# Channel gate of a convolutional block: wider matmuls for the two sums over pixels, and a one-byte throw-away output

## The reference

```
xn   = group_norm(x, 32 groups of 16 channels)
r    = relu(xn)
r    = where(max_pixels(r) - mean_pixels(r) < 0.5, 0, r)
bb   = 1 - exp(-|max_channels(r) - mean_channels(r)|)      # one value per pixel
y    = bb * r
x_max, pooled = max_pixels(y), mean_pixels(y)
c1   = sigmoid(pooled @ W1.T);  c3 = relu(pooled @ W3.T);  c3 = where(c3 < 1, 1.2, c3)
out  = x + where(y < c1 * c3 * x_max, 0, y)
```

## Time and profile before

| | |
|---|---|
| device time, median of 3 runs | 1788.29 us (1784.95 to 1790.47) |
| the profiled execution, its own time | 1780.24 us |
| its span in the trace | 1778.4 us |
| mean granted TensorE clock | 0.843 of 2.4 GHz |
| instructions in the trace | 45243, of these 19616 matmuls and 19616 weight loads |
| mean DMA rate | 292 GB/s |

### The profile page before, as it was taken

How to read it: one execution, slowest core, us unless ns; L and a number is a source line. 1 busy time by engine, 2 the same in 40 slices (tenths; PEclk the granted TensorE clock), 3 DMA queues, 4 the chain that set the end, 5 groups by cost and what they waited for, 6 DMA issues and landing times.

```text
span 1778.4 us, 45243 instructions
## 1 busy us (share of the span) xinstructions
PE 1303.4 (73%) x19616; PEld 1080.2 (61%) x19616; DVE 1460.9 (82%) x2192; ACT 1306.6 (73%) x1921; POOL 610.6 (34%) x446
## 2 busy tenths in 40 slices
PE   4888776788876778767688777678777688777761
PEld 3766655666665666655576655566655566656660
DVE  2588887988887988888888887888887887888987
ACT  5678777777787878777767787777787767777821
POOL 0043233443233444223443233443233442233430
PEclk8898888998888898888888888898878887888885
DMA  9259989999999899998989999989999988899973
GB/s 396 87 162 301 319 315 320 281 296 297 312 330 336 277 285 306 302 329 320 287 263 296 307 330 332 283 277 296 301 330 329 279 265 269 315 329 343 296 228 145
DMA packets 93418, 518.86 MB, mean 292 GB/s; under 512 B 10272, under 2 KB 10272, under 8 KB 93216
## 3 DMA queue, kind: packets, MB, share of 16 engines
q1 hardware_dynamic: 75360, 416.38, 58.4%
q0 software_dynamic: 17856, 99.56, 28.7%
HBM read 310.38 MB, written 205.52 MB: 290 GB/s over the span
## 4 chain that ended last, share of the span: by engine, by line
PE 29%; POOL 26%; ACT 22%; DVE 15%; issue 7%; DMA 1%; SPq 0%; DVEq 0%; ACTq 0%; POOLq 0%
POOL xs L778 23%; ACT rs L476 8%; PE ps_turn L286 7%; PE ps_gate L347 7%; ACT xs L476 7%; PE ps_gate L322 6%; PE ps_gate L294 6%; DVE xs L670 6%; ACT rs L451 5%; DVE rs L670 4%; DVE max_and_mean L622 2%; POOL rstd L757 2%; DMA xs<-in_x 1%; PE ps_gate L356 1%; DVE xs L737 1%
## 5 line engine op out<-in xcount | busy, mean ns | idle before, releaser
L622 DVE TENSOR_REDUCE max_and_mean<-ps_turn 128x2 f32<-128x1024 f32 x384 | 466.0, 1220 | 201.3 <-PE ps_turn L286 200.6
L286 PE MATMUL ps_turn<-ident,xs 128*128 128x128 f32 (+1 forms) x1600 | 358.8, 310 | 177.7 <-DVE max_and_mean L622 112.3
L769 POOL DMA_DIRECT2D xs<-in_x x124 | 111.6, 968 | 940.0 <-DVE xs L670 837.0
L778 POOL TENSOR_TENSOR xs<-xs,rs 128x1568 f32<-128x1568 f32 x124 | 433.3, 3531 | 1.9 <-DVE rs L670 1.9
L286 PEld LDWEIGHTS ps_turn<-ident,xs 128*128 128x128 f32 (+1 forms) x1600 | 204.5, 153 | 311.5 <-DVE max_and_mean L622 155.2
L312 PE MATMUL ps_gate<-ident,bb 128*128 128x128 f32 (+1 forms) x1600 | 273.4, 333 | 153.2 <-ACT bb L469 144.0
L425 ACT ACTIVATE scratch<-xs 128x3136 bf16<-128x3136 f32 x128 | 360.2, 2814 | 7.8 <-DMA xs<-in_x 2.8
L312 PEld LDWEIGHTS ps_gate<-ident,bb 128*128 128x128 f32 (+1 forms) x1600 | 249.6, 239 | 173.4 <-DVE ymax_parts L639 157.7
L286 PE MATMUL ps_turn<-ident,rs 128*128 128x128 f32 (+1 forms) x1600 | 341.3, 299 | 6.0 <-issue 6.0
L639 DVE CUSTOM_DVE_ANT_0 xs<-xs,ps_gate 128x768 f32<-128x768 f32 (+1 forms) x256 | 243.3, 959 | 45.1 <-PE ps_gate L312 45.0
L451 ACT ACTIVATE xs<-xs,shift,rstd 128x3136 f32<-128x3136 f32 x64 | 191.9, 2999 | 100.0 <-POOL shift L761 93.3
(11 more groups left out here) (80 smaller groups left out, 991.9 us busy)
## 6 DMA issues: line engine op xcount, KB each, us to landing
xs<-in_x SPq DMA_DIRECT2D x260, 784.0 KB, 13.7
out<-xs SPq DMA_DIRECT2D x256, 784.0 KB, 8.2
xs<-in_x POOLq DMA_DIRECT2D x124, 784.0 KB, 11.1
rs<-in_L_conv_W SPq DMA_DIRECT2D x2, 1024.0 KB, 18.7
```

The lines of the kernel that those rows point to most:

```text
L286: mm = pe.transpose(ps_turn[0:w, n % 2, b - 2 * i, P * t:P * (t + 1)], r_tile(s, t)[:, P * b:P * b + w], ident[:, :])
L622: ins = dve.tensor_reduce(max_and_mean[:, 2 * i:2 * i + 2, 0], ps_turn[:, n % 2, :, :], AX.X, ALU.max)
L778: pool.tensor_tensor(o, o, half(r_tile(s - 1, t), h), ALU.add).then_inc(added, 1)
```

## The change

`sum_x` takes 448 columns in one matmul instead of 112, so a tile is 7 matmuls and not 28. `mean_rows_of` takes rows of 512 pixels instead of blocks of 128, so a tile is 7 matmuls (the last has 64 columns) and not 25. The four groups of output partitions are used in turn over all 28 matmuls of a sample. Their results lie in the first bank of each half of `ps_gate` or in its second one (`ps_rowsum` in columns 0 to 447 of the second half, `ps_mean_rows` in columns 512 to 1023 of the first), so each step waits for the gates that read these banks, and the wait for `logits_ready` moves from ahead of `sum_x` to `group_stats` and one sample back. `turn_means` becomes four matmuls; ScalarE copies 512 columns of mean rows in place of 128, reads 448 columns of sums in place of 112, and writes the means with a permuted access pattern. `junk` becomes a one-byte tile of its own, and `control_sb` shares memory with the mean rows.

```diff
-XCHUNK = 112
+XCHUNK = 448
+MEAN_ROW = 512
...
-        scratch = sb("scratch", [P, HALF])
-        junk = scratch[:, :].bitcast(BF16)
-        control_sb = scratch[:, 0:C]
+        junk = sb("junk", [P, HW], FP8)
+        rows = sb("rows", [P, C])
+        control_sb = rows[:, :]
+        mean_rows = rows[:, 0:MEAN_ROW]
...
-        ps_mean_rows = small0[:, 0:P]
+        ps_mean_rows = ps_gate[:, 0, 512:512 + MEAN_ROW]
...
-        ps_rowsum = small1[:, 48:48 + XCHUNK]
+        ps_rowsum = ps_gate[:, 1, 0:XCHUNK]
...
             def mean_rows_of(s):
-                for t in range(T):
-                    for b in range(NBLK):
-                        w, k, j = min(P, HW - P * b), b % 4, b // 4
-                        mm = pe.matmul(ps_mean_rows[32 * k:32 * k + 32, 0:w], chan_avg[:, 31 - j:63 - j],
-                                       r_tile(s, t)[:, P * b:P * b + w], start=(t == 0 and b < 4),
-                                       stop=(t == T - 1 and b >= NBLK - 4), skip_group_check=True,
-                                       tile_position=(0, 32 * k))
+                if s > 0:
+                    pe.wait_ge(gated, T * (NG * s - 1))
+                for n in range(T * NM):
+                    t, j, k = n // NM, n % NM, n % 4
+                    w = min(MEAN_ROW, HW - MEAN_ROW * j)
+                    mm = pe.matmul(ps_mean_rows[32 * k:32 * k + 32, 0:w], chan_avg[:, 31 - j:63 - j],
+                                   r_tile(s, t)[:, MEAN_ROW * j:MEAN_ROW * j + w], start=(n < 4),
+                                   stop=(n >= T * NM - 4), skip_group_check=True, tile_position=(0, 32 * k))
                 mm.then_inc(mean_rows_mm, 1)
...
             def turn_means(s):
                 pe.wait_ge(mean_rows_copied, s + 1)
-                pe.matmul(ps_means, mean_rows[:, :], row_block_cols, start=True, stop=True).then_inc(means_mm, 1)
+                for i in range(MEAN_COLS):
+                    mm = pe.matmul(ps_means[:, i, :], mean_rows[:, P * i:P * (i + 1)], row_pick[:, :],
+                                   start=True, stop=True)
+                mm.then_inc(means_mm, 1)
...
             def sum_x(s, tiles):
+                if s > 1:
+                    pe.wait_ge(gated, NG * T * (s - 1))
...
             def group_stats(s):
                 pe.wait_ge(row_mean_ready, s + 1)
+                if s > 1:
+                    pe.wait_ge(logits_ready, s - 1)
...
                 mean_rows_of(s)
-                if s > 0:
-                    pe.wait_ge(logits_ready, s)
...
                 ins = act.activation(junk[:, 0:n], x_tile(s, t)[:, cols], ACT.Square, scale=float(HW) ** -0.5,
-                                     accum_out=squares[:, part:part + 1])
+                                     accum_out=squares[:, part:part + 1], saturate=False)
...
-                act.activation(max_and_mean[:, :, 1], ps_means, ACT.Identity, scale=-1.0).then_inc(means_ready, 1)
+                act.activation(mean_in_place, ps_means, ACT.Identity, scale=-1.0).then_inc(means_ready, 1)
...
             def copy_control(s):
                 act.wait_ge(control_rows, s + 1)
-                junk_step.wait()
```

More of the change, by code:

```diff
@@ L6 @@
 F32 = mybir.dt.float32
-BF16 = mybir.dt.bfloat16
+FP8 = mybir.dt.float8e4
 I32 = mybir.dt.int32
@@ L54, in gated_sparsifier @@
     NX = HW // XCHUNK
+    NM = -(-HW // MEAN_ROW)
+    MEAN_COLS = MEAN_ROW // P
     GROUP_T = (0, 3, 6, 9, NT)
@@ L61, in gated_sparsifier @@
     NS = len(SUMS)
-    assert T == 4 and NBLK == 25 and LAST_W == 64 and NX * XCHUNK == HW and NX % 4 == 0 and GMAX == 832
+    assert T == 4 and NBLK == 25 and LAST_W == 64 and NX * XCHUNK == HW and NM == 7 and GMAX == 832
     x_tiles = x.rearrange("b (t p) h w -> b p t (h w)", p=P)
@@ L90, in gated_sparsifier @@
         chan_avg = sb("chan_avg", [P, 63])
-        row_block = sb("row_block", [P, 7, 4])
+        row_pick = sb("row_pick", [P, NM])
         row_part = sb("row_part", [P, 2])
-        mean_rows = sb("mean_rows", [P, P])
         ones = sb("ones", [P, 1])
@@ L113, in gated_sparsifier @@
         fkeep = sb("fkeep", [P, T])
-        max_and_mean = sb("max_and_mean", [P, NBLK, 2])
+        max_and_mean = sb("max_and_mean", [P, NM * MEAN_COLS, 2])
         diff = sb("diff", [P, NBLK])
@@ L139, in gated_sparsifier @@
         ps_control = ps_logits.rearrange("p (m o) -> p m o", o=T)
-        ps_means = small0[:, P + 4:P + 4 + NBLK]
-        ps_rowsum = small1[:, 48:48 + XCHUNK]
+        ps_means = small0[:, P + 4:P + 4 + NM * MEAN_COLS].rearrange("p (i j) -> p i j", j=NM)
+        mean_in_place = max_and_mean[:, :, :].rearrange("p (j i) c -> p i j c", i=MEAN_COLS)[:, :, :, 1]
+        ps_rowsum = ps_gate[:, 1, 0:XCHUNK]
         ps_control_rows = ps_gate[:, 0, 0:C]
@@ L188, in gated_sparsifier @@
         added_last = sem("added_last")
-        row_block_cols = row_block[:, :, :].rearrange("p j k -> p (j k)")[:, 0:NBLK]
         def x_tile(s, t):
@@ L320, in sum_x @@
                     for c in range(NX):
-                        k = c % 4
+                        q = NX * n + c
+                        k = q % 4
                         mm = pe.matmul(ps_rowsum[32 * k:32 * k + 32, :], sel[:, t, :],
                                        x_tile(s, t)[:, XCHUNK * c:XCHUNK * (c + 1)],
-                                       start=(n == 0 and c < 4), stop=(n == T - 1 and c >= NX - 4),
+                                       start=(q < 4), stop=(q >= NX * T - 4),
                                        skip_group_check=True, tile_position=(0, 32 * k))
@@ L437, in row_means @@
                 steps.step(act.activation(junk[:, 0:XCHUNK], ps_rowsum, ACT.Identity,
-                                          scale=1.0 / (PER_GROUP * HW), accum_out=row_sum[:, :]))
+                                          scale=1.0 / (PER_GROUP * HW), accum_out=row_sum[:, :], saturate=False))
                 steps.wait()
@@ L550, in _ @@
                               AX.XY, ALU.add)
-            dve.tensor_copy(row_block[:, :, :], ident[:, :].rearrange("p (k r) -> p r k", k=4)[:, 0:7, :])
+            dve.tensor_reduce(row_pick[:, :], ident[:, :].rearrange("p (k r) -> p r k", k=4)[:, 0:NM, :], AX.X,
+                              ALU.add)
             dve.tensor_reduce(row_group[:, :], ident[:, :].rearrange("p (a g) -> p g a", g=8), AX.X, ALU.add)
```

## The result

The changed kernel takes 1722.83 us (median of 4 runs, 1721.32 to 1723.58) against 1786.62 us before (4 runs, 1778.93 to 1790.47). The ratio is 0.964, 95% interval 0.9604 to 0.9676. The forecast was 1732 us with a range from 1722 to 1752; the result lies in it, 0.8 us above its lower end. The profiled execution took 1722.46 us with a span of 1720.7 us.

A forecast was written before the change was run, and what follows sets the result against it. A ring of waits with a 51.4 us period, plus TensorE stalls at instruction block ends, bound the kernel; 1780.24 - 50.4 = 1729.8 us, with 2 us staying 1732 us, range 1722 to 1752.

The forecast's parts named there:

- The ring: Wait cycle through GpSimd, ScalarE, TensorE and VectorE from one sample to the next; claimed a period of 51.4 us.
- Fewer instructions, 50.4 us: TensorE's sums and turns: 240 instructions per sample for 852 end the stalls at block ends, worth all 50.4 us.
- The forecast of 77 packets: Sign of being right: TensorE's instruction packets on the instruction queue fall from 154 to about 77.
- The rule against it: Skill text on TensorE's instruction fetch: fetch is hidden, so fewer instructions win nothing and time stays near 1780 us.
- Streaming, 0: TensorE's two sums: time goes by columns, which don't change; 5.4 us each before and after, so 0.
- the rival of lost overlap: TensorE's wide matmuls: only three of four groups overlap, +3.6 us a sample, 1834 us; chance 0.05.
- the prediction's sign of 5.3 to 5.5 us for `sum_x`: Sign of being right: `sum_x` and `mean_rows_of` on TensorE still take 5.3 to 5.5 us each.
- `turn_means`, at most +1.0 us and hidden: TensorE's turns: six more matmul pairs add at most 1.0 us a sample, hidden by ScalarE.
- ScalarE, 0.63 us more, 0.28 left: ScalarE's wider reads ahead of `group_stats`: +0.63 us against 0.9 us to spare, 0.28 left, cost 0.
- One-byte output, 0: ScalarE's squares writing one byte: taken as 0; bounds 0 or 0.19 us slower in each of four squares.
- 2 us of the 8: Profiled execution lies 8 us below the median of the runs; most supposed to be stalls that go, 2 us not.

The follow-up runs named there:

- e10: Changed kernel with four more ScalarE copies of the mean rows ahead of the group statistics: 1824.34 us, ratio 1.0182 to the kernel before.
- e8: Changed kernel with ScalarE's sum of the second gated tile moved ahead of the last relu: 1669.72 us, ratio 0.9365 to the kernel before.
- e7: Changed kernel with one more ScalarE copy of the mean rows ahead of the group statistics: 1721.67 us.
- e1: Changed kernel with the old widths again, 112 columns and rows of 128 pixels, all else kept: 1778.0 us, ratio 0.9929 to the kernel before.
- e2: Changed kernel with half the widening, 224 columns and rows of 256 pixels: 1719.5 us, ratio 0.9605 to the kernel before.
- e3: Changed kernel with rows of 128 pixels in the means alone, sums of x still 448 columns: 1725.36 us, ratio 0.9638 to the kernel before.
- e4: Changed kernel with 112 columns in the sums of x alone, means still rows of 512: 1745.05 us, ratio 0.9734 to the kernel before.
- e12: Kernel before with ScalarE's sum of the second gated tile moved ahead of the last relu: 1821.13 us, ratio 1.0132 to the kernel before.
- e6: Kernel before with the one-byte output of squares and of the read of the sums alone: 1783.15 us, ratio 0.9978.
- e5: Kernel before with loads from the fourth sample on cut to a quarter of their columns: 2172.4 us, with channels masked on old data.
- e9: Kernel before with each store cut to a quarter of its columns: 1781.96 us, ratio 0.9944.
- e11: Changed kernel with 224 columns, rows of 256, the early second gated sum, and GpSimd's last-keep wait moved behind the statistics: 1668.26 us, ratio 0.9316 to the kernel before.

## Why the prediction was right

- **The ring.** 28.93 + 22.4 + 0.08 = 51.4 us was forecast for every sample; 28.92 + 22.2 + 0.08 = 51.2 us is what nearly all have. e10 and e8 moved it both ways.
- **Fewer instructions, 50.4 us.** Shown. The profiled executions differ by 57.8 us. 50.2 of it was the lateness at 17 handovers (the prediction's 50.4, added up from the trace once more), and 6.0 lie in the second segment, from the first control product to the last keep (mean 22.42 us before and 22.22 after, 30 samples each); most of the rest lies in the prologue. The second segment goes with TensorE's clock, as e7 and e10 show; why it was longer before I haven't tested. e1 puts the stalls back with nothing but the widths, e2, e3 and e4 show that they and not the count of matmuls cost the time. The forecast of 77 packets is 78.
- **The rule against it.** The Trainium skill (Runtime: NRT & Kernel Launch, Instruction fetch mechanics) holds that the fetch is hidden. The trace of the kernel before has 47.3 us of stalls at block ends, that of e12 102.1 us in one line alone, so here it is not; the 256-instruction block does agree, with 9824 x 2 instructions over 78 packets, 252 each.
- **Streaming, 0.** The rate is right, 0.218 ns a column, so the four groups overlap as before and the rival of lost overlap did not come. What I had left out: a half of `sum_x` lasts 774.88 - 771.77 = 3.11 us until the next step starts, not 12544 x 0.216 = 2.71, since the last wide matmuls, 0.55 us each, must end first. The two halves together take 6.2 us, and the prediction's sign of 5.3 to 5.5 us for `sum_x` failed. These 0.4 us at each end are hidden under ScalarE.
- **`turn_means`, at most +1.0 us and hidden.** It went from 0.33 to 0.99 us and is hidden; TensorE ended its turns ahead of ScalarE's row means.
- **ScalarE, 0.63 us more, 0.28 left.** The group by line and form of the changed kernel, and ScalarE's timeline:

```profile
L434 ACT ACTIVATE junk<-xs 128x3136 fp8e4<-128x3136 f32 x128 | 360.0, 2813 | 5.2 <-DMA xs<-in_x 1.2 <-issue 0.3
...
L465 ACT ACTIVATE rows<-ps_gate 128x512 f32<-128x512 f32 x32 | 18.6, 581 | 12.3 <-PE ps_gate L298 12.3
...
L446 ACT ACTIVATE junk<-ps_gate 128x448 fp8e4<-128x448 f32 x32 | 17.4, 544 | 3.0
```

```profile
781.34 0.18 ACT L454 ACTIVATE gst<-ps_gate 128x8 f32<-128x8 f32 x1
```

581 ns for 599 assumed and 544 for 555. L454 ends at 781.52, L760 starts at 781.94, so 0.42 - 0.15 = 0.27 us are left. This term was as thin as said, and right.
- **One-byte output, 0.** Shown by e6, and 2813 ns in the change.
- **What was mis-sized** is the step from the profiled execution to the runs. I took 2 us of the 8 between them as staying, and the second segment as unchanged. In fact all of the 8 go: the four runs of the change lie within 2.3 us of each other and around its profiled execution, those of the kernel before within 11.5 us. With the 2 us left out and the 6.0 us of the second segment, for which nothing in the prediction's sum stood, the same working gives 1724 us.
- **Why blocks are late** I did not say in the prediction, and took the bulk of the data as the cause in e5 and e9. For the longer stalls e9 shows that the stores are not it, and e5 speaks against the loads. That the accumulating DMAs are it fits every one of them in time, and is open until a run goes without these DMAs.

## What to carry to other kernels

Where an engine stands at "issue" with nothing to wait for, count its instructions from one such gap to the next. Here a constant count that equals the instructions per packet of the instruction queue meant that it ran out of code, and then fewer, larger instructions helped even though the work that they stream is the same. It was enough to make a block last longer than its successor took to arrive (half the change did). Before an edit to the critical ring, look for such stalls: with them an edit that is worth 3% made the kernel 1% slower, and without them it was worth what the ring said.

## What the hardware showed unexpectedly

- Packets of 16 KB that take no bandwidth to speak of (0.6% of the DMA engines' time) cost 50 us of 1780. In 20 of the 27 stalls of the kernel before, with 42.2 of 47.6 us, the queue of the accumulating DMAs filled the DMA engines, and an instruction packet then started 3.9 us after a block end in place of 1.0. And the stalls go with a wider spread of the time: 11.5 us between the four runs with them, 2.3 between the four without.
- The changed kernel settles to periods of 51.18 to 51.24 us, and 0.11 us more on the ring (e7) left nearly all periods at 51.2 us, since TensorE's clock rose from 1.2 to 2.4 GHz at an earlier point of the control stage. A small delay on such a ring need not show in the time. With a shorter ring (e8, e11) two periods alternate, 48.98 and 50.02 us.
- Four column groups keep their rate from 112 to 448 columns in one matmul (0.216 and 0.218 ns a column), but a stretch ends 0.4 us later.
